# Fourth layer of a mixed transformer: relative attention moved ahead of the switch-head attention, whose value projections change for six of eight heads

## The chip, the cores and the metric

One core of one Trainium2 chip. TensorE (PE) multiplies matrices, its weight loads overlapping them (PEld), VectorE (DVE) and ScalarE (ACT) work on tiles, GpSimd (POOL) computes too and issues transfers of its own, SyncE (SP) issues the other DMAs. The metric is the device time of one execution in microseconds, the median of several; less is better.

## What is computed

Four layers, each `x = x + attention(norm(x)) + ffn(norm(x))`, on x of 4 x 512 tokens x 128 in float32 (16 tiles of 128 tokens). The change touches the fourth, and a little of the third.

```
# relative attention, H = 16 heads of 64, 10 bias buckets, a query sees itself and the 127 keys before it
logits = Q @ K.T / 8 + bias + einsum('bhtn,ntp->bhtp', R, D);  A = softmax(logits) @ V;  out = A @ Wproj + bproj
# switch heads, H = 8 heads of 128, E = 8 experts, the best K = 2 taken for each token and head
gate_v, gate_o = sel(x, sel_v_w), sel(x, sel_o_w)       # [b, s, h, e], two of eight non-zero
xv  = einsum('bsd,hedp->bshep', x, v_w)                 # every expert's value
v   = einsum('bshep,bshe->bhsp', xv, gate_v)
att = softmax(q @ k.T / sqrt(128));  ctx = att @ v
out = einsum('bshep,hepd->bsd', ctx[..., None, :] * gate_o[..., None], o_w)
```

Only two of the eight expert values of a token and head have a weight that is not zero; the output side has the same structure.

## The kernel before

The layer (`layer3`) runs three blocks of engine programs, one behind the other: `norm_and_logits` (normed tokens `xn`, their transpose `xnT`, and the 128 routing logits of a token), `switch_heads`, `relative_heads`. Between blocks every engine waits for all.

**switch_heads** (L2158 on) goes over G = 32 groups, one for a batch and a head, with the head running fastest, each in QT = 4 units of 128 query rows, 128 units in all. `pairs` lists what is filled in each unit: two value fills ("v", for the next group) and two output fills ("y", for the last group), each a 128x512 product of 128 tokens with four experts' weights, so eight "v" and eight "y" for a group. In a unit TensorE does the scores (L2313), one v and one y fill (L2305), four transposes of the probabilities (L2321), once in a group the values product (L2331), then another v and y. `gather` on VectorE adds each quarter of a fill, times the gate of its expert, into `val` or into `x` (L2472): 28 additions for v (four more are done by ScalarE, L2394) and 32 for y in a group. Within one pair a v and a y chain alternate, and each addition waits for the one before it in its chain (`link`). The fills go through a ring of four PSUM banks (`m_full`, `m_free`, `place`).

The gates of a batch come from 21 VectorE steps (`gate_step`) for each side. Batch 0 of the value side is done before the first addition, the rest among the units. `relative_fill` (L2339, L2348) computes the relative terms of the other block: R for four heads at a time, times the buckets; ScalarE negates them into `rows` and SP stores them to `band` in DRAM. `band` has rows of 257, and POOL fills its other 129 columns with 1e9 by 16 transfers of 1032 KB (L2265).

**relative_heads** (L1835 on) has G = 32 groups of two heads. TensorE: scores (L1939), values of the group before the last (L1962), next q and k (L1922), one value fill of the next batch (L1928), transposes (L1948), output products (L1974). VectorE adds scores and `rel` and takes the least (L2088). `rel` is read from `band` by `load_band`, four heads ahead. ScalarE takes exponentials, POOL scales the probabilities (L2058). At the end VectorE adds the output to `x` and SP stores the result.

The second layer's expert block (`sparse_ffn`, L1132 on) sorts tokens by expert into TILES = 39 tiles of 128 slots: POOL scatters rows of `xn` to DRAM by slot numbers (L489), TensorE transposes a tile and multiplies it by weights at an address read into a register (`value_load`), POOL scatters the products (L1166). The first layer reads rows by number (L813).

## Time and profile before

| | us |
|---|---|
| median of 3 runs | 2131.93 (2130.17 to 2134.27) |
| profiled execution: time | 2135.84 |
| profiled execution: span | 2134.1 |
| PE, DVE, ACT, POOL busy | 1922.3, 1526.6, 979.0, 597.8 |
| norm of the fourth layer begins | 998.1 |
| switch_heads, first to last VectorE work | 1015.1 to 1840.8 |
| relative_heads, first PE work to the last addition | 1841.4 to 2131.3 |
| granted TensorE clock, mean | 0.946 |

The page gives busy time by engine, the span in 40 slices of 53 us, and groups of instructions by line. A float32 product of 128x512 stands in the trace as two records of about 0.6 us whose starts are 0.43 us apart, since records overlap; so its cost is read from the distance between starts, not from the mean of a record. The same holds for VectorE: a record of 0.34 us may be followed by the next after 0.26 us.

### The profile page before, as it was taken

The page shows a single profiled execution, that of the slowest core. Times are in us where ns is not written, and L with a number is a line of the kernel's source. Part 1 is how long each engine was busy: PE and PEld are TensorE (multiplying, and loading weights), DVE is VectorE, ACT ScalarE, POOL GpSimd, SP SyncE. Part 2 cuts the span into 40 slices and gives each one's busy share as a digit, 9 for nine tenths or more (in the row PEclk, how much of TensorE's full clock was granted, in tenths as well). Part 3 has the DMA queues.
Part 4 walks back from the last instruction along what each step waited for, and adds up shares of the span by engine and source line. Part 5 has one row for each costly group of instructions (what it writes and reads, how often), then busy time and mean ns, then how long its engine had stood idle before and what let it go on. Part 6 is the DMA issues. An engine that isn't in the chain of part 4 may idle for free. (4 is left out here: it accounts for less than half of the span.)

```text
span 2134.1 us, 31615 instructions
## 1 busy us (share of the span) xinstructions
PE 1922.3 (90%) x9672; PEld 1010.9 (47%) x9672; DVE 1526.6 (72%) x4804; ACT 979.0 (46%) x2285; POOL 597.8 (28%) x1003
## 2 busy tenths in 40 slices
PE   5499998479999958988899999999999999999998
PEld 3233333345555634334344444444444444466666
DVE  6567775566765766997788878878887777755554
ACT  4167665256663426240333333333333333377776
POOL 2556651055552321111000000000000000177777
PEclk9679999589999987998999999999999999999999
DMA  8452222372222020001244444441122211434442
GB/s 280 139 103 35 30 46 38 77 235 55 33 64 47 22 62 21 1 0 47 60 108 109 109 116 103 99 100 60 60 68 65 75 60 40 138 120 124 125 129 79
DMA packets 147357, 175.22 MB, mean 82 GB/s; under 512 B 21460, under 2 KB 124665, under 8 KB 146552
## 3 DMA queue, kind: packets, MB, share of 16 engines
q1 hardware_dynamic: 135672, 148.99, 24.9%
q0 software_dynamic: 11520, 24.21, 5.2%
q8 instruction: 82, 1.34, 0.3%
q14 instruction: 83, 0.68, 0.1%
HBM read 118.64 MB, written 54.51 MB: 81 GB/s over the span
## 5 line engine op out<-in xcount | busy, mean ns | idle before, releaser
L2472 DVE SCALAR_TENSOR_TENSOR x<-f_m,f_gs,x 128x128 f32<-128x128 f32 x1024 | 349.1, 344 | 86.0 <-PE f_m L2305 80.7
L512 DVE TENSOR_REDUCE a_nmax<-a_s 128x1 f32<-128x512 f32 (+3 forms) x512 | 279.2, 585 | 129.3 <-PE a_s L323 67.4
L2472 DVE SCALAR_TENSOR_TENSOR f_val<-f_m,gate,f_val 128x128 f32<-128x128 f32 x896 | 305.4, 343 | 69.0 <-PE f_m L2305 63.3
L2058 POOL TENSOR_SCALAR a_lg<-a_lg,a_rinv 128x256 f32<-128x256 f32 (+1 forms) x256 | 210.7, 843 | 486.3 <-DVE a_rinv L2095 485.9
L2305 PE MATMUL f_m<-f_wv,xn_pair 128*128 128x512 f32 x512 | 263.5, 599 | 4.6 <-DVE f_val L2472 4.6
L2305 PE MATMUL f_m<-f_wo,f_oT 128*128 128x512 f32 x512 | 261.6, 596 | 2.2 <-DVE f_val L2472 1.1
L428 ACT ACTIVATE a_pT<-a_st 128x512 f32<-128x512 f32 (+3 forms) x512 | 229.1, 520 | 36.5 <-PE a_st L349 19.4
L323 PE MATMUL a_s<-t_kp,t_qp 96*128 96x512 bf16 (+3 forms) x512 | 168.3, 364 | 11.9 <-DVEq L496 7.7
L346 PE MATMUL a_st<-t_qp,t_kp 99*128 99x512 bf16 (+3 forms) x512 | 164.5, 357 | 1.2 <-ACT a_pT L428 1.2
L2305 PEld LDWEIGHTS f_m<-f_wo,f_oT 128*128 128x128 f32 x512 | 95.8, 190 | 126.9 <-issue 106.9
L2021 ACT ACTIVATE a_lg<-a_lg,a_nmax 128x256 f32<-128x256 f32 (+1 forms) x256 | 120.9, 476 | 30.8 <-DVE a_nmax L2088 30.8
L2313 PE MATMUL f_s<-xn_pair,f_qT 128*128 128x512 f32 x256 | 134.7, 608 | 0.0
L435 ACT CAST t_qp<-a_m 3x512 bf16<-3x512 f32 x128 | 73.9, 577 | 129.5 <-PE a_m L334 128.8
L2305 PEld LDWEIGHTS f_m<-f_wv,xn_pair 128*128 128x128 f32 x512 | 90.9, 193 | 85.6 <-issue 70.9
L2394 ACT ACTIVATE f_val<-f_m,gate 128x128 f32<-128x128 f32 x128 | 46.9, 367 | 184.0 <-PE f_m L2305 180.3
L361 PE MATMUL a_o<-a_pT,t_vp 128*32 128x512 f32 (+3 forms) x1024 | 116.6, 530 | 15.9 <-ACT a_pT L428 10.8
L2088 DVE CUSTOM_DVE_ANT_0 a_lg<-a_m,a_rel 128x256 f32<-128x256 f32 (+1 forms) x256 | 85.0, 386 | 62.5 <-issue 62.5
L2415 ACT COPY f_pT<-f_t 128x512 f32<-128x512 f32 x128 | 74.9, 585 | 119.4 <-PE f_t L2321 119.1
L2265 POOL DMA_DIRECT2D band<-f_hole x16 | 18.5, 1159 | 391.1 <-PE f_m L2305 391.1
L2331 PE MATMUL f_o<-f_pT,f_val 128*128 128x512 f32 x256 | 115.2, 593 | 0.0
L2321 PEld LDWEIGHTS f_t<-ident,f_prob 128*128 128x128 f32 x512 | 63.8, 141 | 70.2 <-issue 65.9
L477 POOL DMA_INDIRECT yacc<-a_yc,seat x64 | 85.2, 1331 | 23.7 <-DMA yacc<-a_yc,seat 12.8
(395 smaller groups left out, 3480.9 us busy)
## 6 DMA issues: line engine op xcount, KB each, us to landing
a_rel<-band SPq DMA_DIRECT2D x64, 512.0 KB, 4.4
band<-f_hole POOLq DMA_DIRECT2D x16, 1032.0 KB, 9.5
f_wv<-f_wv_in SPq DMA_DIRECT2D x32, 512.0 KB
f_wo<-f_wo_in SPq DMA_DIRECT2D x32, 512.0 KB, 3.5
band<-f_rows SPq DMA_DIRECT2D x64, 256.0 KB, 3.8
w_gate_up<-f_wgu_in SPq DMA_DIRECT2D x4, 1536.0 KB, 13.3
t_qp<-parts SPq DMA_DIRECT2D x192, 32.0 KB
t_kp<-parts SPq DMA_DIRECT2D x192, 32.0 KB
```

The costliest lines, as they stand in the source:

```text
L323: last = pe.matmul(ps[:, 0:n], qp[0:MR, h, qt * P:(qt + 1) * P], kp[0:MR, h, 0:n], start=True, stop=not causal)
L346: last = pe.matmul(out[:, q0:T], kp[0:KT, i % H, kt * P:(kt + 1) * P], qp[0:KT, i % H, q0:T], start=True, stop=not causal)
L361: last = pe.matmul(o_ps[32 * j:32 * j + 32, q0:T], vp[:, g % 4, kt, j, :], pT[:, g % 2, j, begins[kt]:begins[kt] + T - q0], start=(kt == 0 ...
L428: act.activation(pT[:, g % 2, i % 4, begins[kt]:begins[kt] + T - q0], st_ps[w % R][:, q0:T], ACT.Exp).then_inc(exp_done, 1)
L477: pool.indirect_dma_start(yacc[e % 2], bass.IndirectOffsetOnAxis(ap=k.seat[:, 16 * (e % 4) + e // 4:16 * (e % 4) + e // 4 + 1], axis=0), y ...
L512: v.tensor_reduce(nmax[:, h % 4, qt:qt + 1], s_ps[(b * H * QT + u) % R][:, 0:n], AX.X, ALU.max, negate=True)\
L2021: last = act.activation(lg[:, g % 2, half, p, c0:c0 + w], lg[:, g % 2, half, p, c0:c0 + w], ACT.Exp, bias=nmax[:, g % 2, p, qt:qt + 1], sc ...
L2058: last = pool.tensor_scalar(lg[:, g % 2, half, p, c0:c0 + n], lg[:, g % 2, half, p, c0:c0 + n], rinv[:, g % 2, p, qt:qt + 1], None, ALU.mult)
L2305: pe.matmul(ps[:, :], left, w[:, g % 2, i % 2, :], start=True, stop=True).then_inc(full, 1)
L2313: pe.matmul(s_ps[u % 2][:, :], qT[:, g % 2, qt * P:(qt + 1) * P], tokens(g), start=True, stop=True).then_inc(s_done, 1)
L2331: last = pe.matmul(o_ps[:, :], val[:, g % 3, kt, :], pT[:, g % 2, kt, :], start=(kt == 0), stop=(kt == QT - 1))
L2472: ins = v.scalar_tensor_tensor(out, ps[:, e * P:(e + 1) * P], gate, out, ALU.mult, ALU.add)
```

## The change

- **Order.** `relative_heads` runs first, `switch_heads` last and stores the result. The relative terms move into `relative_heads` (three groups ahead); so do all gate steps, now 84 steps on tiles twice as wide, and new routing steps.
- **Holes.** The 1e9 columns of `band` are written from SP in the third layer's scan block; a second buffer of 39 x 128 rows of slots (`spare_rows`) is zeroed there.
- **Heads 0 and 1** keep the v fills as they were ("dense"). The groups now run head by head: group g is head g // 4 of batch g % 4. A head's weights are loaded once.
- **Heads 2 to 7.** For each head POOL scatters 2 x 16 x 128 rows of `xn` into slots sorted by expert (32 indirect transfers), SP loads the 39 tiles in three pieces (`xs`), TensorE transposes each tile ("x" fills) and multiplies it by its expert's 128x128 weights ("z" fills), VectorE copies, SP stores to `yslot`, and POOL fetches for each token its two rows (8 indirect transfers for a group). VectorE combines them with two operations for 128 tokens.

```diff
-def switch_heads(nc, k, tag, d, band, later):
+def switch_heads(nc, k, tag, d, rows, result):
+    H, E, CHUNK, FILLS, RING = 8, 8, TILES // 3, -(-TILES // 4), 3
     G = B * H
+    D = B * DENSE
...
-        pairs[u] = [[f for f in (("v", gv, 2 * r + i), ("y", gy, y0 + i)) if 0 <= f[1] < (G if f[0] == "v" else G - 1)]
+        pairs[u] = [[f for f in (("v", gv, 2 * r + i), ("y", gy, y0 + i)) if 0 <= f[1] < (D if f[0] == "v" else G - 1)]
...
+    slots = {u: [] for u in range(-1, LAST + 1)}
+    for h in range(DENSE, H):
+        names = [("x", h, 0)] + [f for j in range(1, FILLS) for f in (("x", h, j), ("z", h, j - 1))] + [("z", h, FILLS - 1)]
+        first = 4 * (B * h - 5)
+        for i, name in enumerate(names):
+            slots[first + 4 * (i // 5) + min(i % 5, 3)].append(name)
...
+    transfers = [(0, "wo", 0), (0, "wo", 1)] + [(16 * h - 9, "wo", h) for h in range(2, H)]
+    transfers += [(16 * h - 20 if h < DENSE + 2 else 16 * h - 36, "wv", h) for h in range(2, H)]
+    transfers += [(16 * h - 20.5, "xs", h) for h in range(DENSE, H)]
+    transfers += [(u + 1, "store", name) for u, names in slots.items() for name in names if name[0] == "z"]
+    transfers = sorted(transfers, key=lambda t: t[0])
...
+                elif kind == "xs":
+                    sp.wait_ge(sent[i % 2], 16 * 2 * NT * ((i - DENSE) // 2 + 1))
+                    for c in range(3):
+                        if i > DENSE:
+                            filled("x", i - 1, (CHUNK * (c + 1) - 1) // 4)
+                        sp.dma_start(xs[:, CHUNK * c:CHUNK * (c + 1), :], rows[i % 2][CHUNK * P * c:CHUNK * P * (c + 1), :]
+                                     .rearrange("(j p) d -> p j d", p=P)).then_inc(xs_in[c], 16)
                 else:
+                    _, h, j = i
+                    emptied("z", h, j)
+                    n = len(tiles_of(j))
+                    sp.dma_start(yslot[h % 2][4 * P * j:4 * P * j + n * P, :].rearrange("(j p) d -> p j d", p=P), ...)
...
+            def scatter(h, i):
+                if i == 0 and h - DENSE >= 2:
+                    for s in xs_in:
+                        pool.wait_ge(s, 16 * (h - DENSE - 1))
+                for c in range(2):
+                    pool.indirect_dma_start(rows[h % 2], place_of(c, i, h), k.xn[:, i, :], None).then_inc(sent[h % 2], 16)
+            def gather(g):
+                h, b = g // B, g % B
+                if b == 0:
+                    for j in range(FILLS - RING, FILLS):
+                        pool.wait_ge(kept[h % 2][index(h, j) % RING], 16 * stores(h, j))
+                if g >= D + 2:
+                    pool.wait_ge(combined, QT * (g - 1 - D))
+                for i in range(QT):
+                    for c in range(2):
+                        pool.indirect_dma_start(yg[:, g % 2, c, i, :], None, yslot[h % 2], place_of(c, b * QT + i, h))\
+                            .then_inc(got[g % 2], 16)
+            for g in range(D - 9, G - 1):
+                if g + 1 >= D:
+                    gather(g + 1)
+                h, r = (g + 9) // B, (g + 9) % B
+                if h < H:
+                    for i in range(QT * r, QT * r + QT):
+                        scatter(h, i)
...
+            def slot_fill(names):
+                for kind, h, j in names:
+                    if kind == "x":
+                        for c in range(3):
+                            if CHUNK * c in tiles_of(j):
+                                pe.wait_ge(xs_in[c], 16 * (h - DENSE + 1))
...
+                    for n, t in enumerate(tiles_of(j)):
+                        at = slice(n * P, (n + 1) * P)
+                        if kind == "x":
+                            last = pe.transpose(ps[:, at], xs[:, t, :], k.ident[:, :])
+                        else:
+                            last = pe.matmul(ps[:, at], xsT[:, index(h, j) % RING, at],
+                                             wv[:, bass.ds(expert[h, t] + 1024 * (h % 2), P)], start=True, stop=True)
...
+            def combine(g, i):
+                h, t = g // B, g % B * QT + i
+                if i == 0:
+                    v.wait_ge(got[g % 2], 16 * 2 * QT * ((g - D) // 2 + 1))
+                    v.wait_ge(pv_done, g - 2)
+                out = val[:, g % 3, i, :]
+                v.tensor_scalar(out, yg[:, g % 2, 0, i, :], k.share[:, 0, 0, t, h:h + 1], None, ALU.mult).then_inc(weighed, 1)
+                v.wait_ge(weighed, QT * (g - D) + i + 1)
+                v.scalar_tensor_tensor(out, yg[:, g % 2, 1, i, :], k.share[:, 0, 1, t, h:h + 1], out, ALU.mult, ALU.add)\
+                    .then_inc(combined, 1)
```

In the relative block (`r` and `e` are the moved terms, `c` the counts of the routing):

```diff
+    NR, AHEAD, QUADS = 10, 3, B * 4
+    CUTS = (0, 5, 10, 15, GATE)                      # 5 to 6 gate steps of a chain in each of four groups
+    CHAINS = {0: (0, 0), 4: (0, 1), 18: (1, 0), 22: (1, 1)}
+    ROUTE = {8: (0, 6), 9: (6, 12), 10: (12, 1 + NT), 12: (20, 22), ... 17: (33, 33 + ROUTES)}
...
+            relative_rows(0)
+            relative_terms(0)
             fill_qk(("q", 0))
             fill_qk(("k", 0))
+            relative_rows(1)
+            relative_terms(2)
+            relative_terms(4)
...
+                if g + AHEAD < G:
+                    relative_terms(2 * (g + AHEAD))
+                if g % 2 == 0 and g // 2 + 2 < QUADS:
+                    relative_rows(g // 2 + 2)
...
+                for step in gate_steps_at(g):
+                    gate_step(*step)
+                for n in range(*ROUTE.get(g, (0, 0))):
+                    route_step(n)
```

## Rows read from the trace of the kernel before

**Rows 1.** The page: busy time by engine, TensorE's granted clock by slice
```profile
PE 1922.3 (90%) x9672; PEld 1010.9 (47%) x9672; DVE 1526.6 (72%) x4804; ACT 979.0 (46%) x2285; POOL 597.8 (28%) x1003
PEclk9679999589999987998999999999999999999999
```
**Rows 2.** Stages: us, busy (count) by engine, clock, DMA share, GB/s
```profile
1200.20:1703.70 503.50, 501.44 (x1662) 242.16 (x1661) 400.96 (x1405) 183.41 (x414) 10.38 (x9) 1.00 0.31 84
1841.00:1850.00 9.00, 7.87 (x21) 4.11 (x22) 2.70 (x18) 2.37 (x9) 0.00 (x0) 0.50 0.00 1
```
**Rows 3.** Timeline of PE, switch_heads: start, us, engine, line, operation, records
```profile
1299.79 1.16 PE L2348 MATMUL f_m<-f_rel,f_rT 10*128 10x128 f32 x16 [0.34 <-DVE x L2472]
1300.88 1.13 PE L2313 MATMUL f_s<-xn_pair,f_qT 128*128 128x512 f32 x2
...
1303.98 1.02 PE L2305 MATMUL f_m<-f_wo,f_oT 128*128 128x512 f32 x2
1304.84 0.60 PE L2321 MATMUL f_t<-ident,f_prob 128*128 128x128 f32 x4
1305.27 1.02 PE L2305 MATMUL f_m<-f_wv,xn_pair 128*128 128x512 f32 x2
```
**Rows 4.** Timeline of PE: scores of units 0, 28 and 127
```profile
1032.71 1.02 PE L2313 MATMUL f_s<-xn_pair,f_qT 128*128 128x512 f32 x2
...
1200.16 1.13 PE L2313 MATMUL f_s<-xn_pair,f_qT 128*128 128x512 f32 x2
...
1817.48 1.02 PE L2313 MATMUL f_s<-xn_pair,f_qT 128*128 128x512 f32 x2
```
**Rows 5.** Timeline of PE, sparse_ffn: four products of 128x128, then the next tile
```profile
695.54 1.06 PE L1219 MATMUL f_y<-xn_pair,f_hT 128*128 x8
696.44 0.27 PE L1193 MATMUL f_x<-ident,f_rest 128*128 128x128 f32 x1
```
**Rows 6.** Timeline of DVE, last group of switch_heads, where only y is filled
```profile
1805.71 3.06 DVE L2472 SCALAR_TENSOR_TENSOR x<-f_m,f_gs,x 128x128 f32<-128x128 f32 x8 [0.24 <-PE f_m L2305]
1808.68 0.68 DVE L2550 TENSOR_REDUCE f_nmax<-f_s 128x1 f32<-128x512 f32 x1
1809.28 1.50 DVE L2472 SCALAR_TENSOR_TENSOR x<-f_m,f_gs,x 128x128 f32<-128x128 f32 x4
...
1828.07 12.74 DVE L2472 SCALAR_TENSOR_TENSOR x<-f_m,f_gs,x 128x128 f32<-128x128 f32 x44 [0.32 <-PE f_m L2305]
```
**Rows 7.** POOL's indirect transfers: two timeline rows back to back, then lines grouped
```profile
69.20 0.94 POOL L813 DMA_INDIRECT shared<-xrow,token  x1 [0.30 <-issue]
70.45 0.95 POOL L813 DMA_INDIRECT shared<-xrow,token  x1 [0.31 <-issue]
...
L489 POOL DMA_INDIRECT rows<-xn_pair,slot x32: 1000/1007/1051, 439.3 to 533.4; - x32
L1166 POOL DMA_INDIRECT yall<-f_rest,f_owner_row x26: 957/1153/1156, 700.5 to 777.5; - x26
```
**Rows 8.** One line's landing (L1173, two of 832 KB), then DMA issues by line
```profile
DMA to landing us min/median/max: 5.0/6.5/7.9
...
yall<-f_rest,f_owner_row POOLq DMA_INDIRECT x26, 2.4
band<-f_hole POOLq DMA_DIRECT2D x16, 1032.0 KB, 9.5
```
**Rows 9.** Timeline of relative_heads: PE, then DVE's last work of a group
```profile
1961.57 1.79 PE L1939 MATMUL a_m<-a_kT,a_qT 64*128 64x128 f32 x16
1970.15 1.79 PE L1939 MATMUL a_m<-a_kT,a_qT 64*128 64x128 f32 x16
...
1971.12 0.28 DVE L2088 CUSTOM_DVE_ANT_0 a_lg<-a_m,a_rel 128x128 f32<-128x128 f32 x1 [1.80 <-issue]
```
**Rows 10.** Lines of DVE: one gate step
```profile
L2510 DVE SCALAR_TENSOR_TENSOR f_below<-f_below,iota 128x256 f32<-128x256 f32 x16 | 6.2, 419 | 0.1
```
**Rows 11.** Timeline: DVE fills a tile beside POOL's indirect transfers
```profile
66.58 3.47 DVE L907 MEMSET t_qp<- 128x4096 f32 x1 [1.42 <-PEq L593]
```

609 lines of the change are left out of this document (399 added, 210 removed).

## The prediction

> **What bounds the kernel now.** I read the page first, for the engine that is always busy, then the stages of the fourth layer, then the timeline of each engine in one unit, to get costs as distances between starts. The page shows TensorE busy for 90% of the span at full clock nearly throughout [rows 1]. Between units 28 and 108 of switch_heads TensorE is busy for 501.4 of 503.5 us at clock 1.00, VectorE for 401 us, ScalarE for 183 us, POOL for 10 us [rows 2]. A fill, and each other product of 128x512, takes 0.86 us (1303.98 to 1304.84), four transposes 0.43 us, eight small products of the relative terms 1.09 us (1299.79 to 1300.88) [rows 3]. A group has 1 query, 4 scores, 8 v, 8 y and 4 values, 25 x 0.86 = 21.5 us, 16 transposes = 1.7 us and relative terms of 1.09 + 0.43 us: 24.7 us. Units 28 and 127 are 617.3 us apart [rows 4], 24.9 us for four. So TensorE bounds this block, and what leaves it counts in full until another engine is next. The relative block is bound by it too: its groups are 8.58 us apart [rows 9].
>
> **The relative block.** It grows by what moves in: 32 pairs of terms x 1.09 = 35 us and 16 products R x 0.86 = 14 us [rows 3]; the switch block loses the same. The routing counts are 34 narrow products, none of which has a row. From the nearest, a quarter of four 128x128 products (0.22 us [rows 5]), they cost at most 7.5 us, and no less than nothing; I take 2.5. The start now has R, terms, a store of `rows` and a load of the band in a row before the first addition, each transfer some 4 us by the nearest landing of like size, 5.0 [rows 8]; before, the band lay ready. TensorE has about 5 us of its added work meanwhile, so +5 us (0 to 10). Gate steps: 419 ns at 256 wide [rows 10], so about 0.69 us at 512 wide, five in a group, 3.4 us. They stand before the next group's first addition, where VectorE idles 1.80 us [rows 9] and, with the terms that TensorE now does there, 2.9 to 3.9 us. Most are covered; the owner steps of one group (about 4.8 us) are not. +3 us (0 to 30, were the cover gone in all 16 groups). POOL's scaling waits behind nothing new. Together 290 + 35 + 14 + 2.5 + 5 + 3 = 349 us.
>
> **The third layer.** 16 hole transfers of 9.5 us [rows 8] are 152 us if one follows another, beside a scan block of some 180 us that SP otherwise leaves alone: 0, and up to +15 us if they end after it. From the switch block POOL's 16 waits go: nothing, its idle time was free.
>
> **The switch block, TensorE.** It begins without the gate chain: 10 us to unit 0 in place of 17.6 (1015.1 to 1032.7, [rows 4]). Units 0 to 28 took 167.5 us [rows 4]; minus 11 us of relative terms, minus 3 us of early gate steps, plus one head's slots. A head's slots are 39 transposes x 0.107 [rows 3] and 39 products x 0.22 [rows 5], 13 us. Makes 166.5 us. From then no v is filled: 17 x 0.86 + 1.7 = 16.3 us for a group, plus 3.2 us of slots, makes 4.9 us a unit.
>
> **VectorE becomes its equal.** With no v chain beside it the y chain runs bare: eight additions take 2.97 us (1805.71 to 1808.68) [rows 6], where the mixed ones come every 0.26 us. A unit costs 2.97 + 0.60 (maximum, 1808.68 to 1809.28), 0.74 for the two operations of `combine` at the bare distance of 0.37, 0.39 for its share of ten 0.6 us copies in 16 units, 0.1 for scaled gates: 4.8 us, and with a wait of 0.24 [rows 6] 5.05 us. I take 5.05, 81 us for the 16 units of a head, and 4.6 us without slots.
>
> **POOL decides.** It had nothing to do here and now issues 192 scatters and 192 gathers. Back to back one comes every 1.25 us (69.20 to 70.45), 0.95 us of work and 0.30 us of issue; scatters that stand apart take 1.007 and 1.153 us [rows 7]. I take 1.255, the row nearest to eight in a row, and keep 1.45 (1.153 + 0.30) as the other end. From head 2 on POOL's program alternates a gather of 8 and a scatter of 8: 64 for a head, 80 us, against 81 us of TensorE and VectorE. That alone would fit. But it doesn't stand alone: the first gather of head h waits for the last stored product of h; the scatters of h + 2 stand between the gathers of h; SP loads `xs` of h + 2 only when all of these have landed; and x of h + 2 must come 16 units after the end of h. Worse, the load of `xs` (sort key 16h - 20.5) stands in SP's program ahead of the last two stores of head h - 1 (key 16h - 20). So SP sits at the wait for `sent` of head 4 with the last stores of head 3 behind it, and the gather of head 3 waits for these. The heads' chains can't overlap. One turn: 80.3 us for 64 transfers, 3 us for the last to land (2.4 [rows 8]), then 12 us until the stores behind it have landed: three issues, three loads of 832 KB (5.0 us for the first, 3 more for the next [rows 8]), the store. Sum 95.4 us. Between: a store landing independently of the loads gives 6 us in place of 12, and the waits of `gather` for `combined` then hold the turn at 12 units + 1 + 20 + 3 + 5 = 90 us; twice 12 is the other bound.
>
> The Trainium skill (DMA: Bandwidth & Descriptors, Queues, rings and completion order) says that descriptors of one issuing engine's ring are consumed in ring order on each DMA engine. By that rule the stores start behind 2.5 MB of loads, as I took it; without it the turn is the 90 us.
>
> From the end of unit 27: 5 us to the store of head 2, 80.3 + 3 + 5, so head 4's slots open after 93 us, not 81; three more turns of 95.4 open head 7 (unit 92) after 379 us. TensorE and VectorE alone would need 64 x 5.05 = 323. **So 56 us of the gain are lost to waiting at `xs_in`.** TensorE, idle for over 10 us at these, should show clock 0.50 behind them, as it does at the block change (0.50 in 1841 to 1850 [rows 2]); within a turn there is room for that, after the last it costs about 4 us.
>
> **The sum**, against the span of 2134.1 us. The fourth layer's two blocks take 1119.0 us from 1015.1. After: relative 349, change of block 0.6, start 10, units 0 to 28 166.5, 28 to 92 379, 92 to 108 81 + 4, the last 20 units 92, the tail 18.7 (1817.48 to the end of VectorE's last row, 1840.8, less one unit of 4.6 [rows 4, 6]), store 2.8: 1103.6 us. That is 15.4 us less. The profiled execution took 2135.84, 3.9 over the median 2131.93, so I take the difference from the median: **2116 us**.
>
> **Rivals.**
> POOL slower. For: 1.153 us in sparse_ffn, the same scatter of 128 rows [rows 7]. Against: those follow a 2 us wait, and runs of eight should go as L813 does. At 1.45 each transfer adds 0.195 us, 256 of them lie between units 28 and 92: +50, 2166 us. It decides the sign from +0.06 us each, 1.32 us, since 256 x 0.06 = 15. This is the case on the other side.
> POOL not in the way: the chains overlap after all, or the compute engines are slower anyway and take the wait. The 56 us return: about 2066. Against: the order in SP's list.
> Compute slower than either engine's own sum: VectorE and TensorE are within 3% of each other, four banks are a short ring, and the gate steps may delay the additions. 0.4 us more in the 36 units after unit 92 and in 28 before, and 15 us in the relative block: +40, 2150 us.
> POOL held up by VectorE. `combine` multiplies a tile in SBUF: 16 such operations in a turn of about 0.26 us, in which POOL would wait: +4.2 us a turn, +17 in four: 2133 us. A fill of a tile from 66.58 to 70.05 [rows 11] stood beside L813, and the transfer at 69.20 took its 0.94 us [rows 7]; no operation of this form stands beside one.
> By the Trainium skill (SBUF — State Buffer, Who interferes with whom) a VectorE `tensor_scalar` in its two-port mode and GpSimd shut each other out for whole instructions. The trace shows no case of it; it is this last rival.
>
> **How the numbers follow.** Chances: forecast 0.42 (its own range 2095 to 2138), POOL slower 0.25, POOL free 0.13, compute slower 0.12, POOL held up 0.08. The range 2066 to 2170 takes all in down to the edges of the first two rivals. A measurement can tell 0.2%, 4.3 us, from no change. The forecast gives faster 0.34, same 0.04, slower 0.04; POOL slower 0.03, 0.02, 0.20; POOL free all 0.13 faster; compute slower 0.01, 0.02, 0.09; held up 0.02, 0.03, 0.03. Sums: 0.53, 0.11, 0.36.
>
> **What would show it.** Right: POOL busy some 365 us more, its records near 0.95 us; TensorE waiting 10 us or more at the first x fill of heads 4 to 7; heads' slots about 95 us apart; y additions 0.37 us apart; the relative block near 349 us. Wrong: no wait of TensorE at `xs`, transfers of 1.15 us, TensorE waiting for banks that VectorE holds, or a relative block over 370 us.

## The result, and the profile after

| | before | after |
|---|---|---|
| median, us | 2131.33 (2130.17 to 2134.27) | 2339.74 (2337.3 to 2348.37) |
| profiled execution: time, span | 2135.84, 2134.1 | 2337.3, 2335.5 |
| PE, DVE, ACT, POOL busy | 1922.3, 1526.6, 979.0, 597.8 | 1892.4, 1509.2, 972.2, 960.5 |
| granted TensorE clock, mean | 0.946 | 0.901 |

The ratio is 1.0984 (95% interval 1.0964 to 1.1005): the change costs 208 us, where 16 us less were forecast and 2170 us was the upper end of the range. The page of after, TensorE's and POOL's busy share and the clock by slice (58 us each), against [rows 1]:

```profile
PE 1892.4 (81%) x10024; PEld 1038.7 (44%) x10024; DVE 1509.2 (65%) x4344; ACT 972.2 (42%) x2245; POOL 960.5 (41%) x1371
PE   5699995689899589979999953988567767678898
POOL 3466630455423111126677765001345444453331
PEclk8689997799999699989999986999788888888999
```

The relative block ends within the 24th slice. It and the next have TensorE at 5 and 3 tenths, and from the 29th on it is busy for 5 to 8 tenths over nine slices while no other engine is busier. Stages of after (us; busy time and count of PE, PEld, DVE, ACT, POOL; clock, DMA share, GB/s), the first to be laid beside the stages of [rows 2]:

```profile
1011.00:1358.00 347.00, 338.07 (x2530) 227.66 (x2530) 230.96 (x996) 242.44 (x757) 225.98 (x256) 1.00 0.52 153
1380.00:1400.00 20.00, 2.14 (x6) 1.59 (x7) 1.74 (x4) 1.63 (x4) 15.13 (x17) 0.53 0.15 51
1400.00:1420.00 20.00, 2.96 (x5) 0.86 (x3) 3.14 (x8) 0.37 (x1) 15.13 (x17) 0.59 0.62 178
1420.00:1440.00 20.00, 6.23 (x12) 2.75 (x12) 2.09 (x5) 1.27 (x3) 15.19 (x16) 0.67 0.16 53
1470.00:1500.00 30.00, 30.00 (x95) 14.82 (x93) 24.94 (x87) 10.71 (x25) 0.00 (x0) 1.00 0.06 18
1700.00:2100.00 400.00, 283.40 (x975) 155.32 (x973) 211.52 (x593) 92.47 (x202) 192.69 (x201) 0.84 0.29 80
```

From 1380 to 1440, while POOL issues the 64 scatters of heads 2 and 3 one behind the other, TensorE is busy for 11.3 of 60 us, VectorE for 7.0, ScalarE for 3.3, and the DMA engines for 15% to 62%: nothing works but POOL. As soon as POOL has no transfer to issue (1470 to 1500) TensorE is busy for 30.0 of 30 us. The timeline shows what everything waits for. TensorE's rows, then ScalarE's, of after (start, us, engine, line, operation, records, idle time and its cause):

```profile
1374.74 0.60 PE L2679 MATMUL f_t<-ident,f_prob 128*128 128x128 f32 x4
1375.17 1.02 PE L2637 MATMUL f_m<-f_wv,xn_pair 128*128 128x512 f32 x2
1376.03 1.02 PE L2671 MATMUL f_s<-xn_pair,f_qT 128*128 128x512 f32 x2
1376.89 1.02 PE L2637 MATMUL f_m<-f_wv,xn_pair 128*128 128x512 f32 x2
1397.86 1.12 PE L2679 MATMUL f_t<-ident,f_prob 128*128 128x128 f32 x4 [19.94 <-ACT f_prob L2769]
...
1373.68 0.68 ACT L2769 ACTIVATE f_prob<-f_s,f_nmax 128x512 f32<-128x512 f32 x1
1386.04 0.37 ACT L2738 ACTIVATE f_val<-f_m,gate 128x128 f32<-128x128 f32 x1 [11.59 <-remote]
1396.54 0.59 ACT L2762 COPY f_pT<-f_t 128x512 f32<-128x512 f32 x1 [10.13 <-DMA f_owner_row<-table]
1397.02 0.69 ACT L2769 ACTIVATE f_prob<-f_s,f_nmax 128x512 f32<-128x512 f32 x1
```

The four transposes at 1374.74 end at 1375.34 by their records. The copy of their result, which waits for nothing else, starts at 1396.54: **TensorE's signal is 21 us behind its record.** (The trace has the update of the semaphore itself at 1396.52, so it isn't ScalarE that is slow to react. Whether TensorE's work was late too, and not its signal alone, these rows can't tell.) TensorE itself then waits 19.94 us for the exponentials that stand behind this copy. The signals in the other direction are in time (the exponential ends at 1397.71, the next transposes start at 1397.86, right behind its accumulator read). The profile names a DMA and "remote" as the releaser, because by its records TensorE had long been done; there is no such DMA. These are the rows of the list of waits that grow, for 1380 to 2335:

```profile
POOL f_yg L2587 <- DVE f_val L2837: 208.8, 18, 29.8
DVE x L2809 <- remote: 159.3, 24, 14.7
ACT f_pT L2762 <- DMA f_owner_row<-table: 109.7, 18, 10.8
ACT f_oT L2774 <- DMA a_yg<-yacc: 90.3, 13, 9.8
ACT f_xsT L2749 <- remote: 87.4, 11, 11.5
```

POOL is no bound by its own work: it waits 208.8 us for VectorE's combining, and 246.3 us, 181.5 of them before its first gather, for stores of products. And its transfers have the price that was forecast (0.30 us of issue and, as duration min/median/max in ns):

```profile
L2587 POOL DMA_INDIRECT f_yg<-yslot,slot x192: 940/945/1027, 1621.3 to 2290.5; - x192
L2576 POOL DMA_INDIRECT rows<-xn_pair,slot x96: 954/959/1033, 1359.2 to 1998.7; - x96
```

### The profile page after: what moved, and what is told of

Read it like the earlier page. It is cut to its first block and busy times, and to the rows that moved or that the text cites. A ratio compares the mean times of both kernels' runs of the same rounds, so it can differ in the third digit from the quotient of the medians.

```text
span 2335.5 us, 33312 instructions
## 1 busy us (share of the span) xinstructions
PE 1892.4 (81%) x10024; PEld 1038.7 (44%) x10024; DVE 1509.2 (65%) x4344; ACT 972.2 (42%) x2245; POOL 960.5 (41%) x1371
## 3 DMA queue, kind: packets, MB, share of 16 engines
q0 software_dynamic: 19424, 32.49, 5.4%
## 5 line engine op out<-in xcount | busy, mean ns | idle before, releaser
L2809 DVE SCALAR_TENSOR_TENSOR x<-f_m,f_gs,x 128x128 f32<-128x128 f32 x1024 | 353.8, 348 | 266.9 <-remote 159.3
L2587 POOL DMA_INDIRECT f_yg<-yslot,slot x192 | 182.5, 950 | 506.6 <-DMA yslot<-f_ys 246.3
L2637 PE MATMUL f_m<-f_wo,f_oT 128*128 128x512 f32 x512 | 285.8, 645 | 80.9 <-issue 43.2
L2217 POOL TENSOR_SCALAR a_lg<-a_lg,a_rinv 128x256 f32<-128x256 f32 (+1 forms) x256 | 226.0, 902 | 152.1 <-DVE a_rinv L2254 151.6
L2679 PE MATMUL f_t<-ident,f_prob 128*128 128x128 f32 x512 | 85.5, 294 | 72.1 <-ACT f_prob L2769 42.5
L2809 DVE SCALAR_TENSOR_TENSOR f_val<-f_m,gate,f_val 128x128 f32<-128x128 f32 x224 | 74.9, 343 | 80.5 <-remote 40.4
L2247 DVE CUSTOM_DVE_ANT_0 a_lg<-a_m,a_band 128x256 f32<-128x256 f32 (+1 forms) x256 | 85.1, 385 | 42.3 <-issue 42.2
L2853 DVE TENSOR_REDUCE f_nmax<-f_s 128x1 f32<-128x512 f32 x128 | 87.5, 684 | 36.6 <-DMA a_yc<-yrow 27.0
L2576 POOL DMA_INDIRECT rows<-xn_pair,slot x96 | 92.5, 964 | 36.8 <-issue 28.9
L2576 POOL DMA_INDIRECT spare_rows<-xn_pair,slot x96 | 92.5, 963 | 29.2 <-issue 29.2
```

The lines of the kernel that those rows point to most:

```text
L2217: last = pool.tensor_scalar(lg[:, g % 2, half, p, c0:c0 + n], lg[:, g % 2, half, p, c0:c0 + n], rinv[:, g % 2, p, qt:qt + 1], None, ALU.mult)
L2576: pool.indirect_dma_start(rows[h % 2], place_of(c, i, h), k.xn[:, i, :], None).then_inc(sent[h % 2], 16)
L2587: pool.indirect_dma_start(yg[:, g % 2, c, i, :], None, yslot[h % 2], place_of(c, b * QT + i, h))\
L2637: pe.matmul(ps[:, :], left, w, start=True, stop=True).then_inc(full, 1)
L2679: last = pe.transpose(t_ps[:, kt * P:(kt + 1) * P], prob[:, u % 2, kt * P:(kt + 1) * P], k.ident[:, :])
L2809: ins = v.scalar_tensor_tensor(out, ps[:, e * P:(e + 1) * P], gate, out, ALU.mult, ALU.add)
```

## The experiments

An indirect transfer takes the address of each of its rows from a table of numbers; a plain one moves a block. A scatter is an indirect store to DRAM, a gather an indirect load.

The theory that the trace suggests (A): indirect transfers that POOL issues back to back hold TensorE up. The rivals: the reordering itself; the transfers' bytes; the prediction's own chain of POOL and SP, wrongly sized.

**Parts of the change.** `dense8` keeps the new order and fills all eight heads' values as before (`DENSE = 8` within switch_heads).

> The changed kernel with all eight heads' values filled as before: relative block first, groups head by head, routing still computed, but no scatters, no xs, z, yslot, gathers or combine. Reorder theory (the loss is in the reordering itself): near the changed kernel's 2339.7 us. Theory that the indirect transfers of POOL hold TensorE up, and the prediction's own theory too: start 1010.9, relative block 347, 11 us to unit 0, 32 groups of 25 x 0.86 + 1.7 = 23.2 us make 742, tail and store 22, together 2133 us (2120 to 2150), about the time of before, with TensorE busy throughout.

Measured 2117.38 us, ratio 0.9944 (0.992 to 0.9968). The reordering is not the loss; it gives 14 us, where I had expected none. `plain` has the whole change, with each indirect transfer made a plain one of the same size (its numerical result is then another):

```diff
-                    pool.indirect_dma_start(rows[h % 2], place_of(c, i, h), k.xn[:, i, :], None).then_inc(sent[h % 2], 16)
+                    pool.dma_start(rows[h % 2][(2 * i + c) * P:(2 * i + c + 1) * P, :], k.xn[:, i, :]).then_inc(sent[h % 2], 16)
...
-                        pool.indirect_dma_start(yg[:, g % 2, c, i, :], None, yslot[h % 2], place_of(c, b * QT + i, h))\
-                            .then_inc(got[g % 2], 16)
+                        n = 2 * (b * QT + i) + c
+                        pool.dma_start(yg[:, g % 2, c, i, :], yslot[h % 2][n * P:(n + 1) * P, :]).then_inc(got[g % 2], 16)
```

> The changed kernel with each of the 384 indirect transfers replaced by a plain one of the same 64 KB from POOL, in the same place and order and with the same waits (rows then stand unsorted, so the result is another). If the indexed form is what hurts (theory A in its narrow form): the prediction's sum comes true, 2066 to 2130 us. If POOL's issuing of any software transfer hurts, or the chain and SP's order (the prediction's own terms, wrongly sized): near 2339 us.

Measured 2075.67 us, ratio 0.9744 (0.9721 to 0.9766), 264 us less than after. By the starts of the scores, 65 of these lie in units 0 to 28 (243.9 us in after, 178.6 in `plain`) and 194 in units 28 to 92 (523.4 and 329.7). The queue of these transfers has the same 19424 packets and 32.49 MB on both pages, so it is not the traffic. Stages of `plain` at the place of the worst stall of after:

```profile
1400.00:1420.00 20.00, 20.00 (x57) 9.46 (x56) 15.58 (x54) 6.44 (x15) 0.00 (x0) 1.00 0.00 1
1420.00:1440.00 20.00, 20.00 (x65) 9.99 (x64) 16.52 (x58) 7.73 (x18) 0.00 (x0) 1.00 0.09 27
```

A plain transfer also takes POOL 0.54 us in place of 1.26, so `plain` alone doesn't tell the kind of transfer from its rate. The doses do. Nor does TensorE wait for its instructions to be loaded: no packet of the instruction queues starts between 1373.0 and 1431.4 in after, TensorE works again from 1397.86 without one, and both pages have the same 171 of them.

**Doses in an otherwise idle POOL.** Three kernels are `dense8` with 32 transfers at a time that nothing in the kernel waits for. Cost is the time from one start of TensorE's scores to another, over the units of the dose and three behind it, less that of the same units in `dense8`. Each kernel ran once; the doses without a cost agree with `dense8` within 0.1 us.

```diff
+            def dose(kind, h, n, between, buffer):
+                for m in range(n):
+                    c, i = m % 2, m // 2
+                    if kind == "scatter":
+                        pool.indirect_dma_start(rows[buffer], place_of(c, i, h), k.xn[:, i, :], None).then_inc(sent[0], 16)
...
+                    if between(m):
+                        pool.memset(idle[:, 0:between(m)], 0.0).then_inc(paced, 1)
+                        pace[0] += 1
+                        pool.wait_ge(paced, pace[0])
```

> dense8 with six doses of transfers on POOL, which is idle there otherwise; nothing in the kernel waits for them. 32 scatters back to back at unit 6, 32 gathers back to back at unit 24, 32 scatters each followed by a fill of 128x1024 (about 0.95 us) at unit 44, the same with a fill of 128x512 at unit 64, 32 plain (not indirect) stores of 64 KB from POOL at unit 84, 32 scatters with a fill after each eighth at unit 98. Theory A (POOL's indirect transfers back to back hold TensorE up, one weight load or product for each transfer): the first two doses cost some 25 us each (TensorE busy under 5 of 20 us), the spaced doses much less, plain stores nothing or the same as scatters, which tells whether it is the indexed form or POOL's issuing. Theory B (the waiting of the changed kernel's own chain, POOL and SP in turns): no dose costs anything, time as dense8.

> dense8 with six other doses: 32 scatters of rows of 64 bytes back to back at unit 6, 32 scatters of 64 partitions only at unit 24, 32 scatters with a fill of 128x256 after each (about 0.25 us) at unit 42, 32 scatters each issued after the one before has landed at unit 60, 32 scatters with a fill of 128x1024 after each fourth at unit 84, 32 gathers with a fill of 128x1024 after each at unit 104. If bytes matter, the narrow rows cost TensorE little; if the number of descriptors matters, they cost the same as full rows, and 64 partitions half; if only the number of instructions, all the same. Waiting for each landing (about 2.4 us) should cost nothing by theory A. By theory B nothing costs anything.

> dense8 with seven doses of indirect transfers of 128 rows from POOL, which nothing waits for: 32 scatters with a fill of 128x8 after each at unit 6 (POOL waits for its end); the same without that wait at unit 24; a wait that is long met before each at unit 40; a fill of 128x8 after each fourth at unit 58; a fill of 128x256 after each fourth at unit 76; the same after each second at unit 94; 32 gathers with a fill of 128x256 after each at unit 110. If any other work of POOL between two transfers ends what they do to TensorE: only the third dose costs (24 to 29 us as doses1's back-to-back ones), the time is 2142. If the free time between transfers counts: the fills of 128x8 and the fills after each fourth leave a part of it, and more than one dose costs.

| dose of 32 | mean spacing, us | cost, us |
|---|---|---|
| scatters of 64 partitions, back to back | 1.201 | 30.7 |
| gathers, back to back | 1.252 | 28.9 |
| scatters, each behind a wait that is met | 1.262 | 28.7 |
| scatters of 64 bytes a row, back to back | 1.265 | 27.5 |
| scatters, back to back | 1.268 | 29.1 |
| fill of 128x8 after each, not waited for | 1.309 | 27.6 |
| fill of 128x256 after each fourth | 1.332 | 23.1 |
| fill of 128x1024 after each eighth | 1.359 | 17.7 |
| fill of 128x8 after each, waited for | 1.364 | 21.9 |
| fill of 128x8 after each fourth | 1.374 | 19.4 |
| fill of 128x256 after each second | 1.411 | 8.4 |
| fill of 128x1024 after each fourth | 1.476 | 0.0 |
| gathers, fill of 128x256 after each | 1.549 | 0.0 |
| scatters, fill of 128x256 after each | 1.567 | 0.0 |
| fill of 128x512, of 128x1024, or waiting for the landing | 1.86 to 2.60 | 0.0 |
| plain stores of 64 KB | 0.534 | 0.0 |

The times were 2201.14, 2176.09 and 2240.89 us. Bytes don't matter (64 a row cost as much as 512), nor the number of rows, nor the direction; the indexed form and the **rate** do: nothing at 1.48 us and above, 8 us at 1.41, 28 us at 1.26. (Between, the mean spacing is not all: at 1.36 the cost is 17.7 us with one long pause after each eighth transfer and 21.9 with a short one after each.) A row of transfers doesn't begin to cost at once: in `doses1`, whose first dose starts at 1407.1, TensorE is busy without a gap up to 1422, some twelve transfers in. My guess that any other work between two transfers ends it was wrong (the fill of 128x8). A back-to-back dose and a spaced one, in stages of `doses1`:

```profile
1432.00:1437.00 5.00, 0.23 (x1) 0.23 (x2) 0.00 (x0) 1.26 (x3) 3.78 (x5) 0.61 0.15 52
1437.00:1442.00 5.00, 0.89 (x4) 0.48 (x3) 0.00 (x0) 0.00 (x0) 3.78 (x5) 0.50 0.15 52
1700.00:1750.00 50.00, 50.00 (x143) 23.78 (x142) 41.51 (x147) 16.69 (x39) 43.88 (x46) 1.00 0.13 41
1916.00:1932.00 16.00, 16.00 (x46) 7.50 (x45) 12.68 (x45) 4.22 (x10) 16.00 (x31) 1.00 0.39 124
```

In the first two TensorE does next to nothing beside ten transfers; in the third it is busy for 50.00 of 50 us beside 23 transfers and as many fills; in the last beside 31 plain stores.

**Pauses in the changed kernel.** `paced1` fills 128x256 after each transfer, `paced4` after each fourth, `paced4_order` has SP's loads of `xs` behind the last stores of the head before, too.

```diff
+            def pause():
+                n[0] += 1
+                if True:                             # paced4: n[0] % 4 == 0
+                    n[1] += 1
+                    pool.memset(idle[:, :], 0.0).then_inc(paced, 1)
+                    pool.wait_ge(paced, n[1])
...
-    transfers += [(16 * h - 20.5, "xs", h) for h in range(DENSE, H)]
+    transfers += [(16 * h - 19.9, "xs", h) for h in range(DENSE, H)]      # the kernels named _order
```

> The changed kernel, POOL filling 128x256 after each of its indirect transfers and waiting for that. In doses2 transfers spaced in this way were 1.57 us apart and no unit grew. If back-to-back transfers held TensorE up, the signals of TensorE are in time again, and what is left is the prediction's POOL chain: 64 x 1.57 + 15 = 115.5 us for a turn, against 82.5 us in the run with plain transfers (2075.7 us): four turns, +132, about 2208 us. If the chain overlaps more than the prediction had it, down to 64 x 1.57 = 100.5 us a turn: 2148 us. If back-to-back transfers were not the cause: 2340 us or above, since POOL only gets slower.

> The same with the fill of 128x256 after each fourth transfer only, which makes some 1.34 us a transfer. Doses of four in a row with a longer fill behind them had no cost in doses2. By the prediction's chain: 64 x 1.34 + 15 = 100.8 us a turn, 2075.7 + 4 x 18.3 = 2149 us; with full overlap 85.8 us a turn, 2089 us. If TensorE is held up all the same: over 2250 us.

> paced4 with SP's three loads of xs behind the last two stores of the head before in its list, in place of ahead of them. The prediction says that the stores wait behind the loads and cost the turn 12 us where 6 would do, and that the heads' chains can then overlap: turn 100.8 to 95 or less, four times 6 us or more, 24 us less than paced4 (up to 60 less). If SP's order doesn't matter: as paced4 within 4 us.

> paced1 (2212.2 us, heads 117.0 us apart) with SP's loads of xs behind the last two stores of the head before. The prediction's term: the stores land 6 us earlier when they don't stand behind the loads, and the chains of two heads can then overlap until POOL's own 64 x 1.57 = 100.5 us bind: a turn of 100.5 to 111 us, four turns, 2148 to 2188 us. If SP's order doesn't count: 2212 us, 117 us a turn.

`paced1` took 2212.24 us (ratio 1.039, 1.0357 to 1.0423), 4 us from the 2208 of the chain: POOL does more work than in the changed kernel and the kernel is 127 us faster. `paced4` stayed at 2331.76 and `paced4_order` at 2333.44 us, against my expectation and in line with `doses3`: 1.33 us is not enough. `paced1_order` took 2183.2 us (1.0232, 1.0199 to 1.0265), 29 us less than `paced1`: with the hold-up gone, SP's order counts. SP's loads of `xs` for heads 4 to 7 in `paced1`, then in `paced1_order`:

```profile
1662.47 4.66 SPq L2552 DMA_DIRECT2D f_xs<-rows  x3
1779.49 4.57 SPq L2552 DMA_DIRECT2D f_xs<-spare_rows  x3
...
2012.93 4.33 SPq L2552 DMA_DIRECT2D f_xs<-spare_rows  x3
...
1667.68 5.18 SPq L2552 DMA_DIRECT2D f_xs<-rows  x3
1773.43 5.14 SPq L2552 DMA_DIRECT2D f_xs<-spare_rows  x3
...
1985.37 4.46 SPq L2552 DMA_DIRECT2D f_xs<-spare_rows  x3
```

A turn is 117.0 us (1662.47 to 1779.49) and 105.8 us. What makes the difference stands in POOL's and SP's timelines of `paced1` behind the last scatter for head 5, and in POOL's of `paced1_order` at the same place; the last two rows are the waits of `paced1` for `xs`:

```profile
1777.25 0.97 POOL L2586 DMA_INDIRECT spare_rows<-xn_pair,slot  x1 [0.28 <-POOL f_idle L2578]
1794.15 0.98 POOL L2598 DMA_INDIRECT f_yg<-yslot,slot  x1 [15.61 <-DMA yslot<-f_ys]
...
1784.10 2.86 SPq L2545 DMA_DIRECT2D f_wv<-f_wv_in  x1
1787.01 1.18 SPq L2558 DMA_DIRECT2D yslot<-f_ys  x2
...
1772.75 0.98 POOL L2598 DMA_INDIRECT f_yg<-yslot,slot  x1 [0.27 <-POOL f_idle L2578]
...
PEld f_m L2671 <- DMA f_xs<-rows: 56.5, 2, 29.0
PEld f_m L2671 <- DMA f_xs<-spare_rows: 56.3, 2, 28.8
```

POOL stands still for 15.61 us, until the two stores have landed that SP issues at 1787.01 behind the loads of `xs` and of weights; the prediction had 3 + 12 us for this. With the stores ahead it goes on at once. Its 64 transfers are then 100.5 of the 105.8 us, and most of the rest is a wait of 4.6 us for VectorE's combining (1691.75 to 1696.30). In `paced1` TensorE waits for `xs` four times some 28 us.

**Which transfers.** `scatters_only` and `gathers_only` leave one kind indirect and make the other plain, with the lines of `plain`.

> The changed kernel with the gathers alone replaced by plain transfers of the same size from POOL (the values combined are then those of other rows). doses1 gives the price: the first ten or so of a row of back-to-back indirect transfers cost nothing, each further one 1.1 us, 24 us for 32. Here the 64 scatters of the start stand in one row, the later ones in eights between plain transfers: 54 x 1.1 = 60 us above the run with plain transfers, 2136 us. If the loss came from the gathers: about 2076 us. If any one of the two kinds alone holds the whole loss: 2340 us.

> The reverse: the scatters alone replaced by plain stores of the same size from POOL. The gathers stand in eights, each eight behind other transfers or a wait: by the same price nothing, so 2076 to 2090 us. If it is the gathers that cost (they read what TensorE's products left in DRAM, and VectorE waits for them): over 2200 us.

2176.61 and 2120.7 us, 101 and 45 us above `plain`. Together that is 146 of 264 us. My price had 60 and 0: too low for both. In `scatters_only` the 64 scatters of the start took most (TensorE busy for 14.8 of the 60 us from 1380 on). In `gathers_only` even eight gathers in a row have a small price, where I had taken the first ten as free. The other 118 us come only with both kinds together. Two things are then new: the transfers stand in rows of sixteen, and POOL's chain is longer than TensorE's and VectorE's work (57 us by the estimate below). No run splits these 118 us.

**A version that beats both.** `wide3` fills heads 0 to 2 as before and takes five from slots. A third buffer of slots (zeroed in the third layer) lets POOL issue the scatters of four heads ahead of the first gather, those of the last in fours between gathers; 128x256 is filled after each transfer. `wide3_b2b` lacks those fills, `wide2` has six heads from slots.

```diff
+            for h in range(DENSE_HEADS, DENSE_HEADS + 4):
+                for i in range(NT):
+                    scatter(h, i)
+            later = [(h, i) for h in range(DENSE_HEADS + 4, H) for i in range(NT)]
+            for g in range(D, G):
+                gather(g)
+                for h, i in later[0:2]:              # wide2: later[0:2 + g % 2]
+                    scatter(h, i)
+                del later[0:2]
...
+                    if j == 0 and h - 2 >= DENSE_HEADS:          # SP: a head's first store to yslot
+                        for g in (B * (h - 2) + 2, B * (h - 2) + 3):
+                            sp.wait_ge(got[g % 2], 16 * 2 * QT * ((g - D) // 2 + 1))
```

> A version meant to beat both: heads 0 to 2 filled as before, heads 3 to 7 from slots; a third buffer of slots in DRAM (zeroed beside the second), so that the scatters of heads 3 to 6 are all issued ahead of the first gather and those of head 7 in fours between the gathers of heads 3 and 4; POOL fills 128x256 after each transfer. Back-to-back theory with the chain gone: the run with plain transfers (2075.7 us) plus one dense head more, (2117.4 - 2075.7) / 6 = 7 us: 2083 us (2075 to 2100). If spaced transfers still cost something at each, or the chain has another bound than POOL's: 2120 to 2210 us.

> wide3 (2088.9 us) without the fills of 128x256 between POOL's transfers, its order kept: 128 scatters then stand back to back from the start of the block. If the pauses are what saves it: 118 x 1.1 = 130 us lost at the start, and 2 us at each of 20 groups' eight gathers, about 2250 us. If wide3's gain comes from the better order of the transfers and not from the pauses: 2089 us or less.

> wide3 with six heads from slots in place of five: 128 spaced scatters ahead of the first gather (201 us, the first gather is wanted after some 180 to 225 us), 64 more between the gathers. One dense head less gives 7 us: 2082 us; if POOL's 384 x 1.57 = 603 us in 700 are too many and a gather comes late: 2095 to 2130 us.

`wide3` 2088.88 us (0.9798, 0.9768 to 0.9829); `wide3_b2b`, the same without the fills, 2292.65 us (1.0753, 1.0711 to 1.0795): the pauses are worth 204 us, the order of transfers without them (with one dense head more) 47 us against the changed kernel. My price for the rows in `wide3_b2b`, 2250 us in all, was too low again. `wide2` 2078.32 us (**0.9754**, 0.9724 to 0.9784), 53 us under before, 261 under the changed kernel, and 3 above `plain`. Its page:

```profile
PE 1838.2 (89%) x10024; PEld 1018.1 (49%) x10024; DVE 1508.8 (73%) x4344; ACT 970.9 (47%) x2245; POOL 1088.5 (52%) x1755
```

POOL is busy for 128 us more than in the changed kernel, with its fills, and TensorE is back at 89% of a span that is 261 us shorter.

**What is held up.** Four kernels are `dense8` with a block behind it in which TensorE runs series that depend on nothing, beside 48 scatters.

> dense8 with a block behind it in which TensorE runs four series that depend on nothing (64 float32 products of 128x512, 128 of 128x128, 128 bf16 products of 128x512, 128 transposes of 128x128), each first alone and then beside 48 back-to-back scatters, ScalarE noting a signal after every eighth; then VectorE and ScalarE copy 128x512 sixty times each beside 48 scatters, TensorE idle. If TensorE, once held up, gets one weight load or product through for each transfer whatever its size: under the transfers eight products of 128x512 (16 loads and 16 products in the records) take some 40 us in place of 7, eight of 128x128 some 20 us in place of 1.8, and bf16 ones 20 us. If what is held up is TensorE's reading of its operands: the times go with the columns, four times more for 512 than for 128. If only its signals are late and not its work: TensorE's time to the end is the same, and after the last transfer all signals come at once. VectorE and ScalarE: 0.6 us a copy as without transfers, if it is TensorE alone that is hit.

> dense8 with another block behind it: TensorE alone, then beside 48 back-to-back scatters, 64 float32 products of 128x512, then 128 transposes, with one signal at the very end of each series in place of one for every eighth; then, with TensorE idle, sixty ScalarE copies of 128x512, sixty VectorE copies of 128x512, and sixty VectorE scalar_tensor_tensor of 128x128, each beside 48 scatters. If TensorE's work itself is held up: 64 products take 24 us more (79 in place of 55 us, as with a signal for every eighth), the transposes some 100 us more. If only the giving of signals is: 55 and 14 us, or until the transfers end. If ScalarE and VectorE are hit in the same way (each of their operations waits for the signal of the one before): copies 1.3 us apart after the first ten transfers; if it is TensorE alone: 0.65 us and 0.5 us apart throughout.

> dense8 with seven series of TensorE behind it, each beside 48 scatters: (1) 64 products of 128x512 with a signal after each eighth, ScalarE waiting for each and copying; (2) the same, ScalarE waiting only for the last; (3) a signal after 32; (4) 128 transposes, a signal after each eighth, ScalarE waiting for the last; (5) the same, a signal after 64; (6) as (1) and (7) 128 transposes with every signal awaited, but 128x256 filled between the transfers. If the giving of signals is what is slow: (1), (2) 79 us and (4) over 100 us in place of 55 and 14, (3) and (5) hardly more than alone. If it takes an engine that waits and acts on each: (2) and (4) as alone, (1) not. If the pauses between transfers cure it: (6) 55 us, (7) 14 us.

> dense8 and a block behind it with seven series beside 48 scatters each, the first six with the same series run alone directly before (as in probe; in probe3 TensorE had been idle, and nothing was late): (1) 64 products of 128x512, each eighth signalled and awaited; (2) the same, only the last awaited; (3) one signal at the end; (4) 128 transposes, each eighth signalled and awaited; (5) as (1) and (6) as (4), with 128x256 filled between the transfers; (7) as (1), TensorE idle before. If it takes a TensorE that has been at work without a break and signals: (1), (4) are late as in probe (79 and 131 us in place of 55 and 14), (3) and (7) not, (2) tells whether another engine has to wait for each. If pauses cure it: (5) 55 us, (6) 14 us. If probe's lateness had another cause, such as where in the program the series stands: (1) or (4) as alone.

In `probe` the 64 products took 79 us in place of 55, and the 128 transposes 135 in place of 16 (these beside 96 transfers, since the dose meant for the copies started before they had ended). The series wait for nothing, so TensorE's work itself is slowed, not its signals alone. ScalarE's copies, one for each eighth product: the last one alone and the first beside the transfers (which start from 2177.68 to 2237.10), then the third to the sixth; behind them TensorE's records:

```profile
2177.00 0.20 ACT L2927 COPY pr_marks<-pr_mark 128x8 f32<-128x8 f32 x1 [6.67 <-PE pr_ps L2908]
2184.62 0.20 ACT L2927 COPY pr_marks<-pr_mark 128x8 f32<-128x8 f32 x1 [7.43 <-PE pr_ps L2908]
...
2198.36 0.20 ACT L2927 COPY pr_marks<-pr_mark 128x8 f32<-128x8 f32 x1 [6.67 <-PE pr_ps L2908]
2230.27 0.20 ACT L2927 COPY pr_marks<-pr_mark 128x8 f32<-128x8 f32 x1 [31.72 <-remote]
2245.04 0.36 ACT L2927 COPY pr_marks<-pr_mark 128x8 f32<-128x8 f32 x2 [14.57 <-remote]
...
2177.45 38.89 PE L2908 MATMUL pr_ps<-xn_pair,ident 128*128 128x512 f32 x90 [0.49 <-DVE pr_vb L2943]
2217.66 0.59 PE L2908 MATMUL pr_ps<-xn_pair,ident 128*128 128x512 f32 x1 [1.32 <-issue]
2220.47 1.01 PE L2908 MATMUL pr_ps<-xn_pair,ident 128*128 128x512 f32 x1 [2.22 <-issue]
```

The fourth signal comes 31.9 us behind the third. TensorE's records run on to the 45th product (two records each) and then come one record in 2.80 us; at the signal for 32 products it has begun 47. Eight products of 128x128 took up to 37.8 us and eight of 128x512 31.9, so the columns are not what counts; eight transposes took up to 23.1 us, eight bf16 products at most 7.0. The fifth and sixth signal came together, 7 us after the last transfer's record.

It can reach VectorE too. VectorE's sixty copies, each of which waits for the signal of the one before, ran in `probe` beside 48 transfers while TensorE was held up in its transposes, and in `probe2` beside 48 transfers with TensorE idle. The rows of `probe`, then of `probe2`:

```profile
2543.43 11.11 DVE L2950 COPY pr_vb<-pr_va 128x512 f32<-128x512 f32 x22
...
2577.08 0.43 DVE L2950 COPY pr_vb<-pr_va 128x512 f32<-128x512 f32 x1 [0.96 <-DVE pr_vb L2950]
2578.48 0.43 DVE L2950 COPY pr_vb<-pr_va 128x512 f32<-128x512 f32 x1 [0.97 <-DVE pr_vb L2950]
...
2373.32 30.93 DVE L2951 COPY pr_vb<-pr_va 128x512 f32<-128x512 f32 x60
```

In `probe` the first 22 copies came one in 0.51 us and most of the others one in 1.40 us, each of unchanged length; in `probe2` all came one in 0.52 us. So in `probe` an engine's signal to itself was late too. In after this isn't seen: VectorE's additions behind one another stay 0.39 us apart in the stall.

`probe2`, `probe3` and `probe4` were to split this, and in none of them was anything late: 55 to 58 us for the products and 14 to 17 us for the transposes, also in the two series of `probe4` that repeat those of `probe`. ScalarE's and VectorE's operations beside 48 scatters, TensorE idle, were not held up (`probe2`: 0.65 us a ScalarE copy, 0.52 us a VectorE copy, 0.39 us a VectorE addition). So these three say nothing on what pauses cure or signals cost; they show that back-to-back transfers beside a busy TensorE don't always do it. What `probe` has in common with the layer, and they have not, I don't know, nor what in the chip passes the hold-up on. This stays open.

## Why the prediction was wrong, point by point

**The step that failed** is a term put at nothing without a reason: the sum let POOL's transfers cost only POOL's time (80.3 us in a turn) and kept TensorE's and VectorE's 5.05 us a unit beside them. No rival had the transfers slow another engine; the one on VectorE had POOL itself wait. In its place the runs showed that indirect transfers 1.26 us apart stop TensorE: 28 to 29 us for 32 of them where nothing waits for them, some 207 us in the changed kernel. The nearest rows did not show it, and I could have seen that they could not. Of L813's sixteen in a row [rows 7], the first eight stand beside a TensorE without work (busy for 0.00 us from 66 to 76), and `doses1` has no cost in the first twelve or so. The other 58 are 3.0 us apart on average, far above the 1.48 us that turned out to be harmless. A change that put 64 in one row beside an engine busy for 99% was outside all rows, and the range should have said so.

**POOL decides: right, hidden behind the rest.** The price of a transfer (1.255 forecast; 0.945 to 0.959 plus 0.30, and 1.26 between starts) was right, and POOL is busy for 363 us more (365 forecast). The chain was right: at 1.57 us a transfer it makes 64 x 1.57 + 15 = 115.5 us a turn, and `paced1` has 117.0, waits of 28 us at `xs` (10 or more were forecast, with a clock of 0.50 behind them, and 1667 to 1672 has 0.50) and 2212 us where 2208 was worked out. The 15 us behind the last transfer were 15.6. The Trainium skill (DMA: Bandwidth & Descriptors, Queues, rings and completion order) says that descriptors are consumed in ring order on each DMA engine; by that rule the stores start behind the loads. The run in which they no longer stand there agrees, with 11 us less a turn and 29 us less in all (three turns between the four loads, less 5 us by which the first load is later). It doesn't show the rule by itself, since SP's own issues ahead of the stores, 7.5 us, went with the loads. With 1.26 us and no hold-up, the same arithmetic from `plain` gives an estimate of 2075.7 + 4 x (80.3 + 16.5 - 82.5) = 2133 us, which is no change: the 2116 was some 17 us too low even without the failure. So the 208 us come out as -14 for the order, -42 for six heads from slots, +57 for the chain (the estimate) and, as what is left, +207 for the hold-up.

**POOL not in the way: fell as a rival, right as a price.** Its condition, that the chains overlap or the other engines take the wait, did not hold: the estimate gives the chain 57 us, the prediction 56. `plain` makes POOL cheap by force (34 us for what took 80) and took 2075.67. The 2066 that the rival was given is a slip: 2116 less 56, and less the 4 for the clock behind the last wait, is 2056. Against that `plain` is 19 us above. Units 0 to 28 took 178.6 us in place of 166.5, since a head's slots beside v fills cost 2 us a unit, 32 us, where I had 13; units 28 to 92 took 329.7 (323) and 92 to 108 82.9 (81); the units behind them took 6 us less.

**The relative block: right.** 349 forecast, 347.3 measured (first product at 1010.92, last addition at 1357.53 + 0.69). The start to unit 0 too: 10 forecast, 11 measured (1358.54 to 1369.59). The 152 us of hole transfers cost nothing: the first product behind the norm starts at 1010.92, 4 us earlier than before (1015.13).

**VectorE becomes its equal: right.** In after eight y additions take 2.95 us (2281.97 to 2284.92), 2.97 forecast, and in `plain` a unit of the 64 took 5.15 us, 5.05 forecast.

**POOL held up by VectorE: fell** for the changed kernel. The Trainium skill (SBUF — State Buffer, Who interferes with whom) says that a `tensor_scalar` in its two-port mode and GpSimd shut each other out. The gathers beside `combine` took 940 to 1027 ns, the scatters 954 to 1033, no more than those in the dense units, and the stall is worst from 1380 to 1440, where no `combine` runs. Only where VectorE copied 128x512 without a break, in `probe` and `probe2`, were POOL's transfers longer, up to 1.21 us.

**Compute slower, POOL slower (1.45 us): fell.** POOL's records are at their forecast price. Of the first rival only the start came out (units 0 to 28 of `plain` 0.43 us longer each, 0.4 in the rival, by the slots); units 92 to 108 took 5.18 us each where it had 5.45, and the relative block took nothing more. Its time was a slip as well: 2116 and 40 are 2156 us, not 2150.

**The clock.** TensorE's granted clock fell to 0.53 in 1380 to 1400, behind stretches of up to 20 us without work, and the mean over 1700 to 2100 is 0.84, so that a part of the work runs at half rate; this adds to the loss but doesn't begin it: from 1377 to 1380, when TensorE's work has already run out, the clock is still 1.00.

## What to carry to other kernels

Indirect transfers issued back to back from GpSimd are not paid by GpSimd alone: space them beside a busy TensorE, by a small fill (128x256) that is waited for. At 1.57 us 128 in a row cost nothing (`wide2`: units 0 to 28 in 178.5 us, 178.6 in `plain`); 1.48 us was harmless for 32. Spread them over the time that there is by more DRAM buffers. Test an idle engine's new load with a dose that nothing waits for before building on it. When the profile names a DMA or "remote" for waits that grow everywhere at once, compare with the end of the true producer's record.

## What the runs showed of the hardware

- While POOL issues indirect transfers faster than one in about 1.45 us, TensorE's signals reach the other engines later and later (in after, from the record's end: 3.8 us for a v fill, then 7.1 for scores, 11.1 for the next fill, 21.2 for the transposes), and 32 transfers cost up to 31 us. The cost begins between 1.41 and 1.48 us of spacing; at 1.20 to 1.27 us it is 27 to 31 us whatever the rows' size, their number (64 or 128) or the direction. The three blocks of `probe2` to `probe4` were spared, for a reason not found. The last packet of a transfer ends 1.9 us after the start of its record, in the stall as before it (up to 5.4 us beside SP's loads of `xs`), so no queue of transfers builds up.
- In one block (`probe`) VectorE's copies, each waiting for the signal of the one before, came one in 1.40 us in place of 0.52, so the hold-up can reach VectorE's signals too.
- In the stall of `probe` TensorE's records run ahead of its signals by up to 15 float32 products or 31 transposes, and in the products they then come one in 2.80 us: in such a stretch a record's end is not the time at which its result may be used.
- Plain transfers from the same engine, 0.54 us each and one behind the other, have no such cost.
